# Row maxima by sums and sizes of differences for a part of the query tiles

## The reference

```
s = q_h @ k_h.T / sqrt(8)          # 2048 x 2048 per head
p = softmax(s, axis=-1)            # over the keys; causal in L alone
y_h = p @ v_h
```

## Time and profile before

| | |
|---|---|
| median of three runs | 3100.31 us |
| the profiled execution | 3098.8 us |
| its span, first to last instruction | 3096.7 us |
| PE, DVE, ACT, POOL busy | 88%, 69%, 55%, 13% of the span |
| loop over heads in F, from the first Exp on | 527.7 to about 1218 us |
| loop over heads in H | about 2127 to 2830 us |
| mean granted clock of TensorE | 0.904 |

### The profile page before, as it was taken

The page is one execution under the profiler, slowest core; times in us unless marked ns, Lnnn a source line. Parts: engine busy times, 40 slices in busy tenths (PEclk is TensorE's granted clock), DMA queues, the critical chain, the costliest instruction groups (busy, mean ns, idle before and its releaser), DMA issues. The chain is left out here.

```text
span 3096.7 us, 62632 instructions
## 1 busy us (share of the span) xinstructions
PE 2729.7 (88%) x20985; PEld 1185.8 (38%) x20985; DVE 2133.4 (69%) x4020; ACT 1711.1 (55%) x2055; POOL 413.6 (13%) x661
## 2 busy tenths in 40 slices
PE   6788857999999997999599999948999989897998
PEld 2688852223223232444234434422232223233443
DVE  5544457999989895322588777748998989894222
ACT  4222213877777776344156666634777777775433
POOL 1222202111111110000211212111111111110000
PEclk9888856999989999899789999977999999997999
DMA  1000002011101111111211111121111111011111
GB/s 44 1 0 0 0 1 88 28 31 39 40 27 33 40 37 25 67 57 41 80 31 57 49 50 50 50 68 40 40 39 30 30 40 39 25 36 36 69 61 34
DMA packets 86863, 120.25 MB, mean 39 GB/s; under 512 B 16261, under 2 KB 59231, under 8 KB 84223
## 3 DMA queue, kind: packets, MB, share of 16 engines
q1 hardware_dynamic: 80713, 109.35, 11.3%
q10 hardware_dynamic: 5936, 7.66, 0.8%
HBM read 83.40 MB, written 20.55 MB: 34 GB/s over the span
## 5 line engine op out<-in xcount | busy, mean ns | idle before, releaser
L573 DVE TENSOR_REDUCE Hmaxes<-Hm 128x1 f32<-128x512 f32 x1024 | 626.8, 682 | 65.0 <-PE Hm L455 64.9
L573 DVE TENSOR_REDUCE Fmaxes<-Fm 128x1 f32<-128x512 f32 x1024 | 626.7, 682 | 58.2 <-PE Fm L455 57.9
L512 ACT ACTIVATE Hprob<-Hs 128x1024 f32<-128x1024 f32 x512 | 521.8, 1028 | 168.5 <-PE Hs L414 156.7
L512 ACT ACTIVATE Fprob<-Fs 128x1024 f32<-128x1024 f32 x512 | 521.8, 1028 | 161.0 <-PE Fs L414 149.1
L573 DVE TENSOR_REDUCE Lmaxes<-Lm 128x1 f32<-128x512 f32 (+3 forms) x640 | 354.6, 605 | 94.6 <-PE Lm L399 59.9
L512 ACT ACTIVATE Lprob<-Ls 128x1024 f32<-128x1024 f32 (+7 forms) x384 | 293.8, 778 | 166.1 <-PE Ls L414 101.0
L455 PE MATMUL Hm<-Hka,Hqa 60*128 60x512 bf16 x1024 | 292.3, 412 | 52.5 <-DVE Hmaxes L573 26.3
L434 PE MATMUL Fo<-Fprob,Fvh 128*32 128x256 f32 x4096 | 334.0, 405 | 0.3 <-ACT Fprob L512 0.3
L434 PE MATMUL Ho<-Hprob,Hvh 128*32 128x256 f32 x4096 | 331.9, 403 | 0.3 <-ACT Hprob L512 0.3
L455 PE MATMUL Fm<-Fka,Fqa 60*128 60x512 bf16 x1024 | 291.1, 412 | 45.2 <-DVE Fmaxes L573 26.4
L414 PE MATMUL Hs<-Hqa,Hka 60*128 60x512 bf16 x1024 | 248.5, 395 | 0.9 <-ACT Hprob L512 0.9
(11 more groups left out here) (433 smaller groups left out, 3262.1 us busy)
## 6 DMA issues: line engine op xcount, KB each, us to landing
FEwb<-FE_weights SPq DMA_DIRECT2D x8, 1024.0 KB, 5.3
HEwb<-HE_weights SPq DMA_DIRECT2D x8, 1024.0 KB, 5.5
Fvh<-Fvstack SPq DMA_DIRECT2D x17, 256.0 KB, 2.5
Lvh<-Lvstack SPq DMA_DIRECT2D x17, 256.0 KB, 2.5
Hvh<-Hvstack SPq DMA_DIRECT2D x17, 256.0 KB, 2.6
FEw<-in_L_ffn_W SPq DMA_DIRECT2D x16, 256.0 KB, 2.8
HEw<-in_L_ffn_W SPq DMA_DIRECT2D x16, 256.0 KB, 2.9
Fka<-F_kparts SPq DMA_DIRECT2D x34, 96.0 KB
```

The source lines that it names most:

```text
L512: nc.scalar.activation(prob[:, :, :].rearrange("p k q -> p (k q)")[:, lo:hi], sps[n % 2][:, o:o + hi - lo], ACT.Exp, scale=SCALE).then_inc ...
L573: nc.vector.reduce_max(maxes[:, a, t, half:half + 1], src[:, 0:w], AX.X).then_inc(max_free, 1)
```

## The change

In F and H the maximum over two keys is taken as half of their sum plus half of the size of their difference. The keys j and j+512 of each half of 1024 keys form a pair. The projection of k is linear, so POOL forms differences and sums of xT's columns once (half the size is put in by the 0.5 below), and four more blocks go through wk and the splitting; they are stored in a new DRAM tensor and loaded per head into a new tile `pairs`, six transfers in addition to those before. Tiles 2 and 5 of each half are taken so, and in head 0 all eight tiles of the first half.

A paired tile is one entry in the order of the scores (PE: two matmuls of differences into a buffer `s`; ACT: Abs of its 1024 columns into `size`) and two items instead of four (PE: a matmul of sums into a buffer `m`; DVE: one operation that adds `size`, scales and takes the maximum). A head has 36 entries and 58 items instead of 32 and 66. Worked out from the lists, the paired entries of a head stand at positions 0, 11, 17 and 28, three scores before their use; DVE divides in front of the items of entry 18. Between the second score of a head and that place there are 13 scores, 2 differences and 23 maxima (4 of them paired) and a turn, before it were 14 scores and 27 maxima and a turn; from there to the second score of the next head there are 18 scores and 2 differences (before 18 scores), 33 maxima (4 paired) and a turn.

`ka`, `pairs`, `vstack`, `topp` and `nothing` become tiles for the whole kernel and are filled once, by POOL, in the first normalisation ahead of F. The maxima of the first half head come in front of k's arrival; the k parts of F and H are stored last in the set-up and loaded in the next block. DVE's loop body has three heads.

```
+PAIRED_TILES = (2, 5)
...
+    def load_pairs(engine, h, s):
+        for r in range(GROUPS):
+            for a in range(PARTS):
+                lo = 64 * r + FIRST_ROW[a]
+                engine.dma_start(pairs[lo:lo + (PARTS - a) * DH, s, :], pscr[r, 0:PARTS - a, bass.ds(h * DH, DH), :]
+                                 .rearrange("b d t -> d b t")).then_inc(loaded[s], 16)
...
+    BLOCKS = [(2, b) for b in range(NB)] + [(w, b) for w in (0, 1) for b in range(NB)] if PAIRED \
+        else [(w, b) for w in (1, 0) for b in range(NB)]
...
+                        nc.gpsimd.tensor_tensor(xs[:, b // 2, b % 2, :], left, right, ALU.add if b % 2 else ALU.subtract)\
+                            .then_inc(mixed, 1)
...
-                nc.gpsimd.memset(ka[0:32, :, :], -1.0).then_inc(filled, 1)
-                nc.gpsimd.memset(vstack[:, :, :, :], 1.0).then_inc(ones, 1)
-                nc.vector.memset(ka[64:96, :, :], -1.0).then_inc(minus_ones, 1)
...
+                if PAIRED:
+                    store(sp, 2, 0)
+                    store(sp, 2, 1)
+                    sp.wait_ge(stored[2], 32)
+                    load_pairs(sp, 0, 0)
+                    sp.wait_ge(stored[0], 32)
+                    load_q(sp, 0, 0)
+                    store(sp, 1, 0)
+                    store(sp, 1, 1)
+                    sp.wait_ge(stored[1], 32)
...
+                def load(h, s):
+                    load_q(sp, h, s)
+                    if PAIRED:
+                        load_pairs(sp, h, s)
+                    load_k(sp, h, s)
+                    load_v(sp, h, s)
...
                         if not first:
                             sp.wait_ge(weighed, RING + NK * h)
-                        load_q(sp, h + 2, (u + 2) % SLOTS)
-                        load_k(sp, h + 2, (u + 2) % SLOTS)
-                        load_v(sp, h + 2, (u + 2) % SLOTS)
+                        load(h + 2, (u + 2) % SLOTS)
                     if not first and not causal:
                         spread(h - 1)
...
+                def differences(h, s, a, t):
+                    ...
+                    for r in range(GROUPS):
+                        rows = slice(64 * r, 64 * r + ROWS)
+                        last = nc.tensor.matmul(into[:, r * BANK:(r + 1) * BANK], qa[rows, s, qt * P:(qt + 1) * P],
+                                                pairs[rows, s, 0:BANK], start=True, stop=True)
+                    last.then_inc(scored, 1)
...
+                    nc.scalar.activation(size[:, pair_at[key] % 2, :], sps[entry_slot(h, "pair", a, t)][:, :], ACT.Abs)\
+                        .then_inc(expd, 1)
...
+                    if n == "pair":
+                        ...
+                        dve.wait_ge(expd, entry_count(h, ("pair", a, t)) + 3)
+                        dve.sem_inc(both_in, 1)
+                        nc.vector.tensor_tensor_reduce(src[:, :], src[:, :], size[:, pair_at[key] % 2, kb * BANK:(kb + 1) * BANK],
+                                                       0.5, LOWEST, ALU.add, ALU.max, maxes[:, a, t, kb:kb + 1])\
+                            .then_inc(max_free, 1)
...
+                    for c in range(NC):
+                        if c == NC // 2 and not first:
+                            divide(h - 1)
...
+            if fill is not None:
+                @block.gpsimd
+                def _(pool):
+                    for n, (tile, value) in enumerate(fill):
+                        if n:
+                            pool.wait_ge(filled, n)
+                        nc.gpsimd.memset(tile, value).then_inc(filled, 1)
+                    pool.wait_ge(filled, len(fill))
...
+        fill = [(consts[n][:][64 * r:64 * r + 32], v) for n, v in (("ka", -1.0), ("pairs", 0.0)) for r in range(GROUPS)]
+        fill += [(consts[n][:], v) for n, v in (("vstack", 1.0), ("topp", 0.0), ("nothing", 0.0))]
```

## The result

The changed kernel takes 3224.49 us (median of 4 runs, 3217.24 to 3232.1), the kernel before in the same series 3101.87 (3094.44 to 3116.36): 1.039 times as long, 95% interval 1.0344 to 1.0436. The profiled execution took 3221.15 us with a span of 3219.4; before they were 3098.8 and 3096.7. The forecast was 3200, range 3090 to 3250, slower.

What follows compares the result with a forecast made beforehand. PE and DVE were close to full, but SP's late `sums` was to decide: +64 cycle, +36 clock, +14 and -5 constants, +2 set-up, -7 first half heads, -6 end heads, +98 on 3098.8, rounded 3200 us; range 3090 to 3250.

Steps and rivals of the forecast that it cites:

- The six issues, x = 4.1: Issue time x of six pair loads ahead of `spread` in F and H: 4.1 us; `sums` lands 21.2 us after W.
- W: Point when the last weighing of the head before is done and SP starts loads for the head after next.
- The cycle: Per head of F and H, 40.3 + x: 44.4 us against 42.1, +2.3; 28 late divisions, +64.
- the clock: Granted PE clock dips behind every late division in F and H: +1.3 us a head, +36, bounds 0 and +64.
- Constants: Fills moved to GpSimd lengthen F's first normalisation by +14; DVE's memset leaving the set-ups gives about -5 in L.
- Set-up and first half head: F and H: set-up +1 each, k stores queued behind pair loads; first half head -3.6 each, pair operations replacing reductions.
- The pair operation: DVE's fused add-and-maximum, 0.8 us each, 8 a head replacing 16 reductions; DVE gains 3.3 us a head.
- Abs at no cost: ACT: 4 Abs of 1.03 us a head, costed at nothing because ACT idles; 4.1 us a head without that cover.
- the table rival: On ACT, Abs and Exp share no table: loads of 10.2 us a head, 3300 us; chance 0.04.
- Wait stays covered: Rival at the division: six issues under 1.8 us together, wait for `sums` stays covered, 3010 to 3070 us; chance 0.12.
- cheap issues: Rival in SP's queue: six issues near 2 us, cycle 42.3, no change, 3100 to 3140 us; chance 0.15.
- DVE bounds: Rival in the head's second part: 1.4 us per pair operation makes it 23.5, 2.2 more, 3260 us; chance 0.07.

Runs made afterwards that it cites:

- kernel with spare loads: Kernel before plus six spare transfers per head, shaped like the pair loads, ahead of ka's in F and H, into a tile nothing reads: 3229.18 us, ratio 1.0419.

## Why the prediction was right, point by point

- **The six issues, x = 4.1.** Measured 4.13 to 4.19. W to `sums` landed came to 21.3 (19.17 and 2.1) where 21.2 stood; the wait was 4.4 us a head where 5.5 stood. The kernel with spare loads shows that this step alone makes the loss, the one with the loads behind `spread` that without it there is none.
- **The cycle.** In terms of 40.3 + x, x = 0, 4.2 and 8.3 gave 42.83, 48.03 and 51.48, clock losses included: steps of 5.2 and 3.45, not of 4.2 and 4.1. Expected for x = 4.1 was 43.5 + 2.3 + 1.3 = 47.1, so 0.9 a head was missing, 25 us over 28 heads; it is the difference between +119 in the two loops and the +94 forecast (64 + 36 - 6). The range was wide enough for it.
  It is not in W to division but behind it. From the division at 896.40 to the next W, at 923.03, it is 26.63 us where 23.2 and 2.5 for the clock stood. The clock's part is right: in the stretches from 894 to 904 above, PE works 3.57 us at 0.50 and 2.00 us at 0.68, which costs 1.8 + 0.6 = 2.4 us. All 14 late divisions in F have such a dip, as expected; by PE's busy time in them it costs 2.6 us on the mean. Without it 24.2 us are left here, against 1.3 + 0.6 + 21.3 = 23.2; 2.0 of them pass before PE starts (898.43), so its work is 22.2. From a division to the next W at a full clock, in the kernel before and in the one with the pair loads behind `spread`:

```profile
805.81:830.08 24.27, 22.77 (x219) 7.71 (x220) 23.54 (x42) 18.36 (x20) 2.88 (x6) 1.00 0.01 4
```

```profile
815.95:840.56 24.61, 23.03 (x230) 6.61 (x229) 22.16 (x42) 21.61 (x23) 2.86 (x6) 1.00 0.04 12
```

  So the mis-sized term is PE's work from the division to the next W, 22.2 where 21.3 stood: the pairs were to shorten this part of the head by 1 us, and it stayed as it was, although DVE's busy time in it fell from 23.54 to 22.16. Which part of PE's sum is too small is open.
- **Constants.** +16.2 for +14. The length is GpSimd's fills, 23.6 us one after another, as summed; the extra is the end of DVE's subtractions, which waited for them (below). L is 3.7 us shorter, for 5.
- **Set-up and first half head.** -10.8 for both stages together, -5 was forecast. In F the set-up is +0.8 (for +1) and the first half head -6.6 (for -3.6): pair operations run at 0.65 us, where 0.8 was taken, and the table load stands directly ahead of the first Exp, as before, and not ahead of the first Abs. No kernel undid the wholly paired first half alone.
- **The pair operation.** Its rows, start and length, show two instructions that overlap:

```profile
874.53 0.70 DVE L758 CUSTOM_DVE_ANT_0 Fm<-Fm,Fsize 128x512 f32<-128x512 f32 x1 [0.54 <-ACT Fprob L685]
875.14 0.14 DVE L758 DVE_READ_ACCUMULATOR2_ANT Fmaxes<- 128x1 f32 x1
875.14 0.73 DVE L758 CUSTOM_DVE_ANT_0 Fm<-Fm,Fsize 128x512 f32<-128x512 f32 x1
875.79 0.14 DVE L758 DVE_READ_ACCUMULATOR2_ANT Fmaxes<- 128x1 f32 x1
```

  From one to the next it is 0.61 to 0.65 us, no dearer than a reduction of 0.61. By the Trainium skill, VectorE: DVE Perf Modes, section "Two Vector instructions with no wait between them", an accumulator output makes two instructions; the trace agrees (141 ns each), but its price is hidden here.
- **Abs at no cost.** 1023 ns each and no table load between Exps, which ends the table rival. Its cover grows thin with more tiles: with four ACT is 94% busy.
- **The rivals.** "Wait stays covered" and "cheap issues" fell with the 4.13 us; "DVE bounds" with the 0.65.

## What to carry to other kernels

Count the issues on a queue, not their bytes: put the transfer that someone waits for ahead of those that are two heads early, and do so before an engine is relieved, or the relief turns into a longer wait. An engine at 95% with a second at 90% behind it need not be the bound alone; divide its busy time by the cycles to see its own share, and what lies above it. A fill moved "beside idle engines" has to be shorter than the block that hides it.

## What the runs showed of the hardware that was not expected

- DVE's subtractions with two scalars stand still while GpSimd fills SBUF: each time two of them last until the fill ends. In the changed kernel 16 of them took 19.77 us beside fills of 2.7 to 7.4 us (the longest one 7447 ns, vstack's fill 7382), in the second normalisation 4.20; the statistics ahead of them kept their 3.19. Rows of the changed kernel:

```profile
451.07 10.48 POOL L862 MEMSET ka<- 32x6144 bf16 x2 [34.38 <-POOLq L38]
451.11 3.19 DVE L827 BATCH_NORM_STATS2 FN1stats<-x 128x6 f32<-128x128 f32 x16 [3.33 <-PEq L38]
...
456.88 19.77 DVE L837 TENSOR_SCALAR n<-x,FN1mv,FN1inv 128x128 f32<-128x128 f32 x16
461.60 5.43 POOL L862 MEMSET pairs<- 32x3072 bf16 x2
467.08 7.38 POOL L862 MEMSET vstack<- 128x8704 f32 x1
```

  With the fills shared, one small DVE operation stood 2.91 us, until 458.02, where GpSimd's fill of vstack ended at 457.99. The Trainium skill, SBUF — State Buffer, section "SBUF: two separate sides", states that VectorE in some modes and GpSimd take a shared pair of ports for a whole instruction and the other blocks; the trace agrees that one waits out the other (7447 ns beside 7382). In which mode the subtractions run no row shows.
- An issue on SP's queue cost 0.69 us for these patterns, as the mean of 12 transfers (8.29/12) and of 6 with twice the bytes each (4.13/6).
- A long pause of PE did not make for much more work at the low clock. At F's late divisions in the changed kernel, behind pauses of 3.3 to 6.7 us, PE worked 3.4 to 9.4 us at 0.50, 5.2 on the mean; behind the short pauses of the kernel before it was up to 6.8 us. Part of the low stretch lies in the pause itself, as from 894 to 898.43 above.
